# A graph network kernel: rows moved to a mean that carries the bias, two products from one set of turned rows

## The reference

```python
edge_index = jnp.stack([src, dst])
x = _layernorm(x + _L0_gnn_ref(x, edge_attr3_10x16, edge_index, ...))      # v + MLP(segment_sum(edge features))
x = _layernorm(x + _L1_gnn_ref(x, edge_weight, src, dst, ...))  # (x @ Ws.T + bs + h_neigh @ Wn.T + bn) / 2
x = _layernorm(x + _L2_gnn_ref(x, L2_gnn_w_s, L2_gnn_w_n, src, dst))       # relu(x @ w_s + agg)
x = _layernorm(x + _L3_gnn_ref(x, edge_index, ...))             # two Chebyshev convolutions, 128 -> 256 -> 128
```

## Time and profile before

| what | value |
|---|---|
| median of 3 runs | 4638.28 us (4631.76 to 4641.12) |
| profiled execution | 4677.37 us |
| its span (first to last instruction) | 4675.5 us |
| mean granted TensorE clock | 0.859 of full |
| busy share of the span | PE 71%, DVE 66%, ACT 53%, POOL 68% |
| `src0`, first to last y0 of POOL | about 700 to 1060 us |
| `nodes` | about 1100 to 2450 us |

### The profile page before, as it was taken

The page is one execution under the profiler, slowest core; times in us unless marked ns, Lnnn a source line. Parts: engine busy times, 40 slices in busy tenths (PEclk is TensorE's granted clock), DMA queues, the critical chain, the costliest instruction groups (busy, mean ns, idle before and its releaser), DMA issues.

```text
span 4675.5 us, 74892 instructions
## 1 busy us (share of the span) xinstructions
PE 3326.4 (71%) x20670; PEld 2625.1 (56%) x20670; DVE 3077.4 (66%) x12829; ACT 2499.1 (53%) x7360; POOL 3168.9 (68%) x3630
## 2 busy tenths in 40 slices
PE   2278977777999999999995655657868867821111
PEld 0135646666888888888884554654436667721111
DVE  2398978997888888888884665771223435545545
ACT  0005668997888888888884551114546633311111
POOL 6405658876888888888884554646656646566666
PEclk6598888999999999999997777888989989955555
DMA  0005544663222222222222433445657756633222
GB/s 21 4 6 171 171 134 167 216 215 107 78 76 76 78 78 74 78 78 74 78 74 81 123 121 100 135 126 177 225 183 263 267 198 211 219 103 92 87 84 75
DMA packets 311878, 575.84 MB, mean 123 GB/s; under 512 B 69502, under 2 KB 97975, under 8 KB 311466
## 3 DMA queue, kind: packets, MB, share of 16 engines
q1 hardware_dynamic: 235178, 443.56, 28.3%
q0 software_dynamic: 76288, 127.51, 10.1%
HBM read 301.23 MB, written 271.14 MB: 122 GB/s over the span
## 4 chain that ended last, share of the span: by engine, by line
DVE 41%; issue 17%; PE 16%; another core or an unknown queue 13%; POOL 6%; ACT 5%; DMA 1%; DVEq 0%; SPq 0%; ACTq 0%; POOLq 0%; PEldq 0%; PEld 0%
DVE bn L969 11%; DVE y L1023 5%; DVE mv L974 4%; PE ps L1444 3%; POOL rows L563 3%; DVE u L1037 3%; DVE y L1043 2%; POOL out_dram L678 2%; DVE x L853 2%; DVE x3b L853 2%; PE ps L1383 2%; PE ps L1426 1%; PE ps L1401 1%; PE ps L1427 1%
## 5 line engine op out<-in xcount | busy, mean ns | idle before, releaser
L563 POOL DMA_INDIRECT rows<-state,rows_of_src x588 | 555.9, 945 | 408.2 <-issue 163.8
L853 DVE TENSOR_TENSOR_SCAN x<-same,x,ps 128x512 f32<-128x512 uint8 x336 | 429.2, 1277 | 354.5 <-remote 238.9
L1401 PE MATMUL ps<-ident,rows 128*128 128x128 f32 x1372 | 289.4, 318 | 421.4 <-ACT rows L1154 248.4
L1137 ACT ACTIVATE yTa<-ps 128x512 f32<-128x512 f32 x392 | 233.0, 594 | 611.1 <-PE ps L1383 308.7
L563 POOL DMA_INDIRECT rows<-lap,rows_of_lap x392 | 380.3, 970 | 215.7 <-issue 107.9
L1401 PEld LDWEIGHTS ps<-ident,rows 128*128 128x128 f32 x1372 | 203.7, 166 | 476.0 <-issue 251.6
L647 POOL DMA_INDIRECT lk<-node_table,look_idx x392 | 390.6, 997 | 91.9 <-issue 87.7
L1142 ACT ACTIVATE sd<-mv,consts 128x4 f32<-128x4 f32 x588 | 174.6, 297 | 493.6 <-remote 176.3
L1540 PE MATMUL ps<-V,hT 128*128 128x128 f32 x3136 | 405.4, 283 | 8.7 <-ACT hT L1273 8.7
L969 DVE BATCH_NORM_STATS2 bn<-y 128x6 f32<-128x128 f32 x1764 | 380.4, 280 | 23.5 <-POOL y L599 23.4
L1540 PEld LDWEIGHTS ps<-V,hT 128*128 128x128 f32 x3136 | 368.0, 193 | 46.0 <-ACT hT L1273 42.8
(11 more groups left out here) (269 smaller groups left out, 9346.7 us busy)
## 6 DMA issues: line engine op xcount, KB each, us to landing
state_h<-hb SPq DMA_DIRECT2D x98, 512.0 KB
xin<-in_x_dram SPq DMA_DIRECT2D x196, 256.0 KB
out_dram<-outb SPq DMA_DIRECT2D x196, 256.0 KB
xe<-state SPq DMA_DIRECT2D x147, 256.0 KB
state<-outb SPq DMA_DIRECT2D x98, 256.0 KB
state<-oe SPq DMA_DIRECT2D x98, 256.0 KB
h_pre<-hb SPq DMA_DIRECT2D x49, 512.0 KB
rows<-in_edge_attr_10x_dram SPq DMA_DIRECT2D x48, 320.0 KB
```

The costliest lines, as they stand in the source:

```text
L563: gp.indirect_dma_start(out=dest[:, at, k, 0:width], out_offset=None, in_=table_, in_offset=bass.IndirectOffsetOnAxis(ap=index[:, c:c + 1] ...
L853: v.tensor_tensor_scan(t[0:np_, g.b].rearrange("p k d -> p (k d)"), same[0:np_, 512 * g.c:512 * g.c + 512], ps[0:np_, bk + g.b, :], t[0:np ...
L1401: i = t.transpose(bank(g.b)[:, k, :], rows[:, g.r, k, 0:P], ident[:, :])
```

## The change

The rows y0 are shifted by sd0 - mean, so that their mean is sd0 instead of the mean of the input. The new first weights are `A1b` = A1 + b1c/128 (in every row). The product then is y0 @ A1 + sd0 * b1c, which is sd0 times the old y1: the bias comes out of the product, and the division by sd0 is left out, because the layer norm behind it cancels a factor (its epsilon is scaled to match: `EPS6`, `tq2`). The second product is made from the same turned rows with `AWb` = A1b @ ws. So y1 exists only in PSUM, it is not turned, and `yTb` and the four instructions of L1023 are gone.

In `nodes` the shift is a broadcast add on DVE in place (`y0_moved`). y0 gets four buffers, POOL makes it one turn earlier, and PE turns it one turn later. relu of the second product becomes an instruction of ACT (`u2_half`), and DVE adds bank 3 to it. The squares are taken from PSUM after `u2_made`. On ACT the three roots stand ahead of `hT`. In `src0` the shift isn't needed as a step of its own: the normalized rows `outb` of the first layer, made as y0 * rs0 + `lift`, are what PE turns, and DVE does both relu and add. `src0` keeps products of two blocks in PSUM (`PRODUCTS`). The setup makes A1b and AWb in two more small steps. The loops lose one tail turn in places. The core of the diff:

```diff
+A1b, AWb = sb("A1b", [P, P]), sb("AWb", [P, P])
...
-EPS4, EPS1, EPS2, HALF = (consts[:, n:n + 1] for n in range(4))
+consts = sb("consts", [P, 5])
+EPS4, EPS1, EPS2, HALF, EPS6 = (consts[:, n:n + 1] for n in range(5))
...
+y0_ring = (y0[:, 0], y0[:, 1], y1[:, 0], y1[:, 1])
...
+PRODUCTS = ((3, 4), (7, 1))
...
     def make_y0(p, g):
-        (x_in if p == "nodes" else x_gathered).wait(pool, p, g)
-        y0_turned.wait(pool, p, g, back=2)
+        if p == "nodes":
+            x_in.wait(pool, p, g)
+            y0_turned.wait(pool, p, g, back=RING)
+            gp.tensor_tensor(y0_ring[g.r], xin[:, g.b], all4(c0h[:, :]), ALU.add).then_inc(y0_made.sem, 1)
+            return
+        x_gathered.wait(pool, p, g)
         bn0.wait(pool, p, g, back=2)
-        if p == "src0":
-            x1_most.wait(pool, p, g, back=2)
-            x1_made.wait(pool, p, g, back=2)
+        x1_most.wait(pool, p, g, back=2)
+        x1_made.wait(pool, p, g, back=2)
         gp.tensor_tensor(y0[:, g.b], xin[:, g.b], all4(c0h[:, :]), ALU.add).then_inc(y0_made.sem, 1)
...
-            next_, g2, g3 = g.less(-1), g.less(2), g.less(3)
+            next_, g2, g3 = g.less(-2 if p == "nodes" else -1), g.less(2), g.less(3)
...
-                rs0.wait(pool, p, g)
+                off1.wait(pool, p, g)
                 out_st.wait(pool, p, g, back=2)
-                gp.tensor_scalar(outb[:, g.b, 3, :], y0[:, g.b, 3, :], mv[:, 0, g.b, 3, 0:1], rs[:, 0, g.b, 3:4],
-                                 ALU.subtract, ALU.mult).then_inc(x1_made.sem, 1)
+                y0_turned.wait(pool, p, g, back=2)
+                gp.tensor_scalar(outb[:, g.b, 3, :], y0[:, g.b, 3, :], rs[:, 0, g.b, 3:4], lift[:, g.b, 3:4],
+                                 ALU.mult, ALU.add).then_inc(x1_made.sem, 1)
...
+        v.scalar_tensor_tensor(A1b[:, :], b1c[:, :], 1.0 / P, bank(6)[:, 0, :], ALU.mult, ALU.add).then_inc(vstep, 1)
+    def rows_turned():
+        dve.wait_ge(tstep, T_ROWS)
+        v.tensor_copy(Bm, bank(6)[:, 1, :]).then_inc(vstep, 1)
+    def rows_times_ws():
+        dve.wait_ge(tstep, T_PRODUCT)
+        v.tensor_copy(AWb[:, :], bank(6)[:, 2, :])
+    weights_at = {64: weights_alone, 68: weights_turned, 76: weights_folded, 84: weights_last,
+                  92: rows_turned, 100: rows_times_ws}
...
-                p1_made.wait(dve, p, g)
-                y1_turned.wait(dve, p, g, back=2)
-                squared.wait(dve, p, g, back=2)
-                if not nodes:
-                    x2_made.wait(dve, p, g, back=2)
-                for k in range(4):
-                    i = v.scalar_tensor_tensor(y1[:, g.b, k, :], bank(3)[:, k, :], dev(0, g.b, k), b1c[:, :],
-                                               ALU.mult, ALU.add)
-                i.then_inc(y1_made.sem, 1)
...
+    def moved(g, out_ap):
+        return v.tensor_tensor(out_ap, sd[:, 0, g.b, :], mv[:, 0, g.b, :, 0], ALU.subtract)
+    def src0_turn(g):
+        p, n = "src0", QUADS
+        g1, g2, g3 = (g.less(k) for k in (1, 2, 3))
+        i0, i1, i2, i3 = (t.inside(n) for t in (g, g1, g2, g3))
+        if i0:
+            y0_made.wait(dve, p, g)
+            stats(0, y0[:, g.b], bn0)
+            bn0.wait(dve, p, g)
+            x1_made.wait(dve, p, g, back=2)
+            aggregate(0, g.b, mv0)
+        if i2:
+            sd2.wait(dve, p, g2)
+            x3_made.wait(dve, p, g2, back=2)
+            v.reciprocal(rs[:, 2, g2.b, :], sd[:, 2, g2.b, :]).then_inc(rs2.sem, 1)
+        if i0:
+            sd0.wait(dve, p, g)
+            v.reciprocal(rs[:, 0, g.b, :], sd[:, 0, g.b, :]).then_inc(rs0.sem, 1)
+            moved(g, lift[:, g.b, :]).then_inc(off0.sem, 1)
+        if i2:
+            rs2.wait(dve, p, g2)
+            v.tensor_tensor(off3[:, g2.b, :], negm[:, g2.b, :], rs[:, 2, g2.b, :], ALU.mult).then_inc(off2.sem, 1)
+        if i0:
+            rs0.wait(dve, p, g)
+            off0.wait(dve, p, g)
+            v.tensor_tensor(lift[:, g.b, :], lift[:, g.b, :], rs[:, 0, g.b, :], ALU.mult).then_inc(off1.sem, 1)
+            off1.wait(dve, p, g)
+            out_st.wait(dve, p, g, back=2)
+            y0_turned.wait(dve, p, g, back=2)
+            for k in range(3):
+                i = v.tensor_scalar(outb[:, g.b, k, :], y0[:, g.b, k, :], dev(0, g.b, k), lift[:, g.b, k:k + 1],
+                                    ALU.mult, ALU.add)
+            i.then_inc(x1_most.sem, 1)
+        if i1:
+            own, near = PRODUCTS[g1.b]
+            p1_made.wait(dve, p, g1)
+            x3_made.wait(dve, p, g1, back=2)
+            v.tensor_scalar(u2[:, g1.b], bank(near), 0.0, None, ALU.max).then_inc(u2_half.sem, 1)
+            u2_half.wait(dve, p, g1)
+            v.tensor_tensor(u2[:, g1.b], bank(own), u2[:, g1.b], ALU.add).then_inc(u2_made.sem, 1)
+            u2_made.wait(dve, p, g1)
+            stats(1, u2[:, g1.b], bn2)
+            bn2.wait(dve, p, g1)
+            aggregate(1, g1.b, mv2)
+            mv2.wait(dve, p, g1)
+            v.tensor_scalar(negm[:, g1.b, :], mv[:, 1, g1.b, :, 0], -1.0, None, ALU.mult)
+            squared.wait(dve, p, g1)
+            v.scalar_tensor_tensor(tmpv[:, g1.b, :], ssum[:, g1.b, :], EPS / P, mv[:, 1, g1.b, :, 1],
+                                   ALU.mult, ALU.add).then_inc(tv2.sem, 1)
+            sd1.wait(dve, p, g1)
+            v.reciprocal(rs[:, 1, g1.b, :], sd[:, 1, g1.b, :]).then_inc(rs1.sem, 1)
+        if i3:
+            h_made.wait(dve, p, g3)
+            h_st.wait(dve, p, g3, back=2)
+            v.tensor_tensor(hb[:, g3.b], wide(5), all4(gb1_row[:, :]), ALU.add).then_inc(h_biased.sem, 1)
+    def nodes_turn(g):
+        p, n = "nodes", BLOCKS
+        g1, g2, g4, g5 = (g.less(k) for k in (1, 2, 4, 5))
+        i0, i1, i2, i4, i5 = (t.inside(n) for t in (g, g1, g2, g4, g5))
+        y0_now = y0_ring[g.r]
+        if i0:
+            y0_made.wait(dve, p, g)
+            stats(0, y0_now, bn0)
+            bn0.wait(dve, p, g)
+            aggregate(0, g.b, mv0)
+        if i2:
+            sd2.wait(dve, p, g2)
+            x3_made.wait(dve, p, g2, back=2)
+            v.reciprocal(rs[:, 2, g2.b, :], sd[:, 2, g2.b, :]).then_inc(rs2.sem, 1)
+        if i5:
+            sd3.wait(dve, p, g5)
+            out_made.wait(dve, p, g5, back=2)
+            v.reciprocal(rs[:, 3, g5.b, :], sd[:, 3, g5.b, :]).then_inc(rs3.sem, 1)
+        if i0:
+            sd0.wait(dve, p, g)
+            moved(g, rs[:, 0, g.b, :]).then_inc(off0.sem, 1)
+        if i5:
+            rs3.wait(dve, p, g5)
+            v.scalar_tensor_tensor(off3[:, g5.b, :], mv[:, 2, g5.b, :, 0], -1.0, rs[:, 3, g5.b, :],
+                                   ALU.mult, ALU.mult).then_inc(off3_made.sem, 1)
+        if i0:
+            off0.wait(dve, p, g)
+            v.tensor_tensor(y0_now, y0_now, rs[:, 0, g.b, :].unsqueeze(2).to_broadcast([P, 4, P]), ALU.add)\
+                .then_inc(y0_moved.sem, 1)
+        if i1:
+            look_in.wait(dve, p, g1)
+            v.tensor_scalar(looked[:, bass.ds(g1.lin(1), 1), :].rearrange("p a c -> p (a c)"), lk[:, g1.b, :],
+                            1.0, None, ALU.mult).then_inc(looked_up.sem, 1)
+            u2_half.wait(dve, p, g1)
+            v.tensor_tensor(u2[:, g1.b], bank(3), u2[:, g1.b], ALU.add).then_inc(u2_made.sem, 1)
+            u2_made.wait(dve, p, g1)
+            stats(1, u2[:, g1.b], bn2)
+        if i4:
+            p3_made.wait(dve, p, g4)
+            x3b_made.wait(dve, p, g4)
+            out_made.wait(dve, p, g4, back=2)
+            v.tensor_tensor(y3[:, g4.b], bank(7), x3b[:, g4.b], ALU.add).then_inc(y3_made.sem, 1)
+        if i1:
+            squared.wait(dve, p, g1)
+            v.scalar_tensor_tensor(ssum[:, g1.b, :], mv[:, 0, g1.b, :, 1], EPS * P, ssum[:, g1.b, :],
+                                   ALU.mult, ALU.add).then_inc(tq2.sem, 1)
+            bn2.wait(dve, p, g1)
+            aggregate(1, g1.b, mv2)
+        if i4:
+            y3_made.wait(dve, p, g4)
+            stats(2, y3[:, g4.b], bn3)
+        if i1:
+            mv2.wait(dve, p, g1)
+            tq2.wait(dve, p, g1)
+            v.tensor_scalar(negm[:, g1.b, :], mv[:, 1, g1.b, :, 0], -1.0, None, ALU.mult)
+            v.scalar_tensor_tensor(tmpv[:, g1.b, :], ssum[:, g1.b, :], EPS / P, mv[:, 1, g1.b, :, 1],
+                                   ALU.mult, ALU.add).then_inc(tv2.sem, 1)
+        if i4:
+            bn3.wait(dve, p, g4)
+            aggregate(2, g4.b, mv3)
...
-                keep(p, g1, y1T_kept, y1_turned, [(p2_made, 1)], yTb[:, :, :], 1)
...
+    def square(p, g, made, source):
+        made.wait(act, p, g)
+        tv2.wait(act, p, g, back=2)
+        squared.wait(act, p, g, back=1)
+        for k in range(4):
+            i = a.activation(unused[:, k, :], source[:, k, :], ACT.Square, accum_out=ssum[:, g.b, k:k + 1])
+        i.then_inc(squared.sem, 1)
+    def src0_turn(g):
+        p, n = "src0", QUADS
+        g1, g2, g3, g4 = (g.less(k) for k in (1, 2, 3, 4))
+        if g1.inside(n):
```

(103 more changed lines are left out.)

331 lines of the change are left out of this document (93 added, 238 removed).

## The result

| | before | after |
|---|---|---|
| median, same chip | 4635.02 us (4627.45 to 4641.12) | 5056.41 us (5047.17 to 5076.53) |
| ratio | | 1.0916, 95% interval 1.0876 to 1.0956 |
| profiled execution, its span | 4677.37, 4675.5 | 5047.17, 5045.4 |
| first to last y0 of `src0` (48 periods) | 700.3 to 1052.0, 7.33 a turn | 684.1 to 1094.4, 8.55 a turn |
| first to last y0 of `nodes` (195 periods) | 1091.3 to 2443.3, 6.93 a turn | 1145.6 to 2846.0, 8.72 a turn |

Slower was forecast, at 4780 us and at most 4950; it is 5056. `nodes` took 348 us more (98 forecast) and `src0` 59 more (44 forecast). The spans differ by 370 us: all that lies outside these two stretches was 37 us shorter in this execution.

A forecast was written before the change was run, and what follows sets the result against it. A DVE and ACT loop with PE nearly full was taken to bound nodes, POOL src0. Nodes +98, src0 +44 and setup +1 gave +143 us on the profiled execution, +142 on the median: 4780 us, range 4735 to 4835.

The forecast's parts named there:

- its y0 ends 3.0 later: In nodes, POOL reaches x3 at about 0.8, starts by 1.27, and ends y0 at 4.27 at the latest.
- Nodes, new walk: Turn in nodes goes from 7.00 to 7.50 us, negm held until POOL's x3b ends; 196 x 0.50 = +98 us.
- The part without the port: In nodes, from the end of y0's aggregate through hT and V to y3's start: 3.65 us.
- That POOL is held by DVE no row here shows: The skill says both engines can block; the trace shows only DVE blocked. By that rule only POOL's x3 shifts.
- Waits until the whole back-to-back run is over: A DVE instruction on SBUF operands coming during POOL's elementwise work waits for the run's end; negm took 1.73 us.
- Src0: In src0, ACT's squares wait for this turn's product and DVE's add: 8.30 us against 7.40, 49 x 0.90 = +44 us.
- (b): Rival: POOL wins at x3 in nodes and DVE stands until 3.3; 9.1 us a turn, 5090 us; chance 0.13.
- (a): Rival: the port costs nothing; nodes 7.07 us a turn, +14, src0 +44, 4697 us; chance 0.15.
- (d): Rival: faster, no port wait, PE's 6.85 us is the period in nodes, src0 at 7.40; 4610 us; chance 0.10.
- PE's loop as it was walked: In nodes, PE's own loop of transposes, products, V and G was summed to 6.85 us a turn.

The follow-up runs named there:

- e1: The changed kernel with the loads of x in nodes issued one turn earlier in SP's list; 4323.55 against 4191.73 us, ratio 1.0322.
- e2: The kernel before with only its loads of x in nodes issued one turn later; 4350.33 us, ratio 1.0388.
- e5: The changed kernel with loads of x a turn earlier and the src0 pass of the kernel before; 4749.43 us, ratio 1.0157.
- e6: As e5, with x3b between the two small transfers of look in POOL's list instead of ahead of both; 4827.3 us, ratio 1.0319.
- e8: As e5, with negm and tmpv in nodes moved behind the statistics of the next y0 on DVE; 4242.81 against 4186.18 us, ratio 1.0132.
- e7: As e5, with DVE's new add in nodes cut from 512 columns to 4, leaving out the rows' shift; 4756.75 us in one run.
- e9: As e5, with hT ahead of sd0 instead of behind it on ACT in nodes; 4738.65 against 4678.70 us, ratio 1.0135.
- e12: As e9, with the shift written to a free PSUM bank, so DVE's add has one operand there; 4141.39 against 4187.94 us, ratio 0.9889.
- e10: As e9, together with the later negm and tmpv of e8; 5119.35 us, ratio 1.0947.
- e4: The changed kernel with the squares and sd1 in src0 moved behind x3 and hb on ACT; 4592.27 us, ratio 1.0969.

## Why the prediction was wrong

**The step that failed** is a wait that the walk put at nothing. It has POOL reach x3 at 0.8 and lets y0 follow at once ("its y0 ends 3.0 later"). In after y0 stood 4.42 us for its load in the turn shown, 402 us in all. The new y0, made a turn earlier, was walked on POOL, DVE and PE, but not through SP's queue. With y0 a turn earlier and its load where it was, the slack of the load (issued at 1709.16 in the kernel before, for a y0 at 1714.51) turned into a wait behind the output's store. It costs 8.72 - 7.24 = 1.48 us a turn, 290 us in `nodes`; e1 gives that back with two lines of SP's list, and e2 makes a wait of the same kind in the kernel before.

**Nodes, new walk**: right as a mechanism once the loads are early. 7.50 was forecast, 7.24 to 7.29 measured in e1 and e5, with x3b after y3 and negm held to its end. The oversize lies behind the hold. negm came 0.89 us into x3b (0.84 forecast) and ended with it, so its own 0.15 us was part of the 0.41 and 0.26 us were hold. The walk starts negm only after x3b (5.82) and adds 1.68 from there, its own time included; from negm's end to the aggregate it was 1.53 in e5, and y3 to the aggregate 3.65 us instead of 3.85. e6 shows that the hold is on the path (+0.48 held, +0.41 a turn), e8 that taking it away gives 0.25 in its own part of the turn. The part without the port was called 3.65 and measured 3.67.

**"That POOL is held by DVE no row here shows"**: rows of after do, x3 at 2.23 us. The longer x3 cost nothing in e1 and e5, where y3 set the turn (e7), and became the bound in e9. The Trainium skill, "SBUF — State Buffer", section "SBUF: two separate sides", has the lock taken by a VectorE instruction with two SBUF inputs; e12 agrees, since one operand in PSUM frees POOL. The same section of the Trainium skill has the loser blocked for the whole instruction: in e9 x3's first instruction lost 0.49 us where 0.61 us of the add was left, most of it.

**"Waits until the whole back-to-back run is over"** holds for some instructions only. `looked` and `negm`, copies and products with one SBUF operand, waited for the end of the run (1.92 us in e10, 1.73 in the earlier trace rows). The add with two SBUF operands did not: in after it began at 2012.41, 1.24 us into x3, took its usual 0.68 us, and the last of x3's four instructions took 0.94 us instead of 0.44. What makes the difference no run tested.

**Src0**: 8.30 was forecast, 8.03 measured where the products ran at full clock. The relu on DVE took 0.69 (0.68 assumed), the squares from PSUM to x3 1.38 against 1.50 from SBUF, and yTa came 0.95 us after hb's start, not 1.04. The clock was left as it was, and from the eighth turn on that was wrong by 0.75 us a turn. The two errors have opposite signs, so it is partly luck that the 59 us lost lie as near the 44 forecast as they do. The Trainium skill's smaller fixed cost of ScalarE from PSUM ("VectorE: DVE Perf Modes", the TRN2 errata) gave an estimated 0.17 us for the squares; 0.12 is measured to the instruction behind them, and the starts of two squares lie 0.25 us apart where they lay 0.29.

**Rivals.** (b), 5090 us, came near in time for another reason. POOL was ahead of the add in after as (b) has it, 1.24 us in the turn shown, but y0 did not follow x3 at once, for it waited for its load, and the add was not held. `looked` was held, over 1 us in 51 of the 170 turns from the 21st on; but the long turns with such a hold have a median of 9.8 us and those without one 10.9, so it is not what made them long. In e10 the hold did set the turn. (a), 7.07, needed the port to be free. (d) was a faster `nodes` at 6.85 with PE as the bound; e12 comes to 6.65, below PE's loop as it was walked, with POOL's list without a wait and PE busy 95%: the change's idea holds room that its order and one operand gave away.

**What stays open**: why the clock falls in the new src0. PE is busy 4.96 us in the turn of 8.03 shown and was busy 4.98 in the mean of two turns of 7.37 before, so its share is lower, and it pauses longer. In after there are 30 pauses of 2.0 us or more from 740 us on; in before there is one from 780 us on, and the clock stayed at 1.00. e4 has PE's work in turns of 8.20 us, hardly a pause of 2.0 us, and a clock of 0.94 against 0.89, so the length of the turn alone doesn't explain it. That the pauses are the cause was not tested.

## What to carry to other kernels

When a step is moved a turn earlier, walk every queue that feeds it: a load that stands behind another transfer's wait in an in-order list inherits that wait, and the profile shows it as an engine idle "until DMA" with all engines below 80%. An elementwise VectorE operation that runs beside GpSimd can be given one operand in PSUM where a bank is free; it was worth 0.55 us a turn here (e12 against e9). With several loops within a few tenths of a microsecond, a repair of one shows next to nothing until the next is repaired too (e7 gained 0.01 us a turn and e9 0.05, the two together 0.56), so test a suspected cost where it is the bound.

## What the hardware showed that was not expected

- GpSimd's four instructions of 128x128 went from 1.73 to 2.23 us beside a VectorE add of 128x512 with both operands in SBUF, and stayed at 1.73 beside the same add with the second operand in PSUM.
- A copy of 4 columns was held 1.92 us, over the last piece of one GpSimd operation and the whole of the next. Two kernels that differ only in the place of two small VectorE instructions (e9, e10) took 7.20 and 9.15 us a turn; in the one VectorE's add comes 0.13 us ahead of GpSimd's x3, in the other 0.84 us behind.
- From the issue of a 256 KB load to the start of the instruction that waited for it went 2.97 us.
- TensorE's granted clock was 1.00 for a whole turn and 0.54 in the products of the next, in a pass with PE pauses of 2.0 to 2.4 us. The price was 0.75 us a turn of 8.03.
